# Attention plus FFN on one core: score matmuls in four column tiles, scores computed further ahead, row maxima turned by TensorE

## The reference

```python
xn = layernorm(x)                                  # x: (2, 1024, 128)
Q, K, V = heads(xn @ wq.T), heads(xn @ wk.T), heads(xn @ wv.T)   # 16 heads of 8 channels
Q, K = rope(Q), rope(K)
scores = where(causal, (Q @ K.T) / sqrt(8), -inf)  # 1024 x 1024 for each of 32 (batch, head) pairs
attn_out = (softmax(scores) @ V) -> (2, 1024, 128) @ wo.T
ffn_out = (xn @ CB.T) * (SCB / 127) + bias
y = x + attn_out + ffn_out
```

## Time and profile before

| | us |
|---|---|
| median of 3 runs | 286.92 |
| lowest, highest | 285.4, 288.29 |
| profiled execution | 285.84 |
| its span, first to last instruction | 284.1 |

### The profile page before, as it was taken

How to read it: one execution, slowest core, us unless ns; L and a number is a source line. 1 busy time by engine, 2 the same in 40 slices (tenths; PEclk the granted TensorE clock), 3 DMA queues, 4 the chain that set the end, 5 groups by cost and what they waited for, 6 DMA issues and landing times.

```text
span 284.1 us, 6851 instructions
## 1 busy us (share of the span) xinstructions
PE 254.6 (90%) x1734; PEld 111.1 (39%) x1760; DVE 217.6 (77%) x618; ACT 186.5 (66%) x350; POOL 108.0 (38%) x179
## 2 busy tenths in 40 slices
PE   0695849679999999999999999999999999998984
PEld 0342815333334334432433343334334432464553
DVE  5898368999898888979897898889888979732123
ACT  0326343566778868787777777687868786677851
POOL 6616999838625104500430043025104500640020
PEclk9999799999999999999999999999999999999996
DMA  7514767400660500150033004200500000001011
GB/s 200 179 35 132 212 132 151 119 2 4 141 155 25 155 16 1 45 125 1 0 85 85 0 1 119 51 0 10 157 4 0 1 1 0 3 20 39 18 39 37
DMA packets 22614, 17.76 MB, mean 63 GB/s; under 512 B 4148, under 2 KB 21940, under 8 KB 22600
## 3 DMA queue, kind: packets, MB, share of 16 engines
q1 hardware_dynamic: 22024, 17.00, 23.6%
q10 hardware_dynamic: 576, 0.59, 0.9%
HBM read 12.12 MB, written 5.24 MB: 61 GB/s over the span
## 4 chain that ended last, share of the span: by engine, by line
PE 77%; DVE 8%; DMA 4%; SPq 3%; issue 2%; POOL 2%; ACT 1%
PE psV L841 25%; PE psB L817 24%; PE psA L796 21%; DVE prod L665 4%; PE psA L891 3%; DMA k_scratch<-ot 2%; SPq L273 2%; DMA x_sb<-x 1%; DVE xn L623 1%; SPq L287 1%; DMA ks<-k_scratch 1%; PE psA L910 1%; PE psB L778 1%; DVE prod L650 1%; DVE stats L613 1%
## 5 line engine op out<-in xcount | busy, mean ns | idle before, releaser
L665 DVE CUSTOM_DVE_ANT_0 prod<-psA,cmask 128x128 f32<-128x128 f32 (+7 forms) x256 | 180.5, 754 | 34.4 <-PE psA L796 32.9
L564 ACT ACTIVATE ring<-psB 128x512 f32<-128x512 f32 x288 | 156.6, 602 | 53.7 <-PE psB L817 52.5
L796 PE MATMUL psA<-ks,qs 128*128 (+4 forms) x375 | 88.3, 327 | 9.3 <-DVE mx L665 5.9
L433 POOL TENSOR_SCALAR_AFFINE_SELECT ring<-ring 128x512 f32<-128x512 f32 x64 | 42.1, 670 | 138.5 <-ACT ring L564 138.3
L817 PE MATMUL psB<-qs,ks 128*128 (+4 forms) x367 | 92.6, 326 | 1.6 <-issue 1.1
L841 PE MATMUL psV<-ring,va 128*32 128x512 f32 (+3 forms) x768 | 78.5, 496 | 0.6 <-ACT ot L571 0.6
L817 PEld LDWEIGHTS psB<-qs,ks 128*128 (+1 forms) x384 | 33.2, 97 | 69.9 <-issue 28.7
L796 PEld LDWEIGHTS psA<-ks,qs 128*128 (+1 forms) x384 | 33.1, 98 | 40.2 <-DVE mx L665 11.1
L841 PEld LDWEIGHTS psV<-ring,va 128*32 128x32 f32 x768 | 16.8, 108 | 29.7 <-issue 19.2
L665 DVE DVE_READ_ACCUMULATOR2_ANT mx<- 128x1 f32 x256 | 21.3, 83 | 0.0
L713 DVE TENSOR_TENSOR xn<-psA,x_sb 128x256 f32<-128x256 f32 x6 | 2.5, 425 | 16.1 <-PE psA L910 16.1
(11 more groups left out here) (80 smaller groups left out, 153.4 us busy)
## 6 DMA issues: line engine op xcount, KB each, us to landing
qs<-q_scratch SPq DMA_DIRECT2D x48, 96.0 KB
ks<-k_scratch SPq DMA_DIRECT2D x48, 96.0 KB
q_scratch<-ot SPq DMA_DIRECT2D x20, 128.0 KB, 2.4
k_scratch<-ot SPq DMA_DIRECT2D x12, 128.0 KB, 2.4
x_sb<-x SPq DMA_DIRECT2D x4, 256.0 KB, 4.8
rope_sb<-rope SPq DMA_DIRECT2D x2, 512.0 KB, 6.2
qs<-shiftsT SPq DMA_DIRECT2D x64, 2.0 KB
y<-xn SPq DMA_DIRECT2D x8, 128.0 KB, 1.8
```

The costliest lines, as they stand in the source:

```text
L433: pool.affine_select(out=view, in_=view, compare_op=ALU.is_ge, fill=0.0, base=0, pattern=[[0, QUAD], [1, P]], channel_multiplier=-1).then_ ...
L564: act.activation(ring[:, s % P_RING, k * HALF:(k + 1) * HALF], bank_b(n % B_RING), ACT.Exp)\
L665: last = dve.tensor_tensor_reduce(masked_scores[:, u % 2, at:at + w], psA[:, (u % 2) * SEQ + at:(u % 2) * SEQ + at + w], cmask[:, SEQ - w: ...
L796: mm = pe.matmul(psA[:, (u % 2) * SEQ + at + k:(u % 2) * SEQ + at + min(k + HALF, w)], stack(qs, i, j, t * P, P), stack(ks, i, j, k, min(H ...
```

## The change

- Each score tile, in `scores` and in `shifted`, is no longer one matmul with 128 columns of weights but four with 32, each into its own 32 output partitions (`score_tile`), the same streamed operand four times.
- `UNIT_BANK` is new: the first three units of a quad come before the first bank of the quad before it (for quad 1 they stand in the prologue), the last comes after bank 28 in place of 34. `VALUE_BANK`, `LAST_VALUE_BANK`, `TASKS`, `TASK_AFTER` and `EARLY` are new too.
- The maxima are turned by a float32 matmul against the identity, with the 16 columns of `mx` as weights. It takes a place of its own in the ring of `psB` banks after banks 13 and 33 (`turn_in_ring`); ScalarE copies the 16x128 result out (`save_maxima`); GpSimd splits it with two operations in place of three; two DMAs in place of four store it. The VectorE transpose goes. Minus one stands in the key stack in place of a negated maximum. For quad 0 two tasks do the turning.
- No engine has a hardware loop any more: every program is written out for all eight quads, and every wait has a constant.
- In the prologue GpSimd fills the pads of slot 2 and the mask before the late rotations; the split of late parts 6 and 7 moves into quad 0; the addition of the FFN result moves from quad 0 to quad 1, in four pieces.

```diff
-UNIT_BANK = [1, 2, 4, 6, 7, 9, 10, 12, 14, 15, 15, 19, 20, 21, 23, 24, 25, 26, 27, 30, 32, 34]
-VALUE_BANK = [9, 14, 17, 20, 23, 25, 31, 35, 39, 42]
-LAST_VALUE_BANK = [9, 12, 14, 17, 20, 24, 28, 33, 37, 39]
+UNIT_BANK = [-5, -3, -1, 0, 3, 4, 5, 9, 10, 10, 11, 13, 13, 16, 18, 20, 20, 22, 23, 24, 27, 28]
+MAXIMA_BANK = [13, 33]
+VALUE_BANK = [10, 13, 16, 20, 23, 27, 31, 36, 40, 43]
+LAST_VALUE_BANK = [10, 12, 15, 20, 22, 25, 28, 33, 37, 39]
-EARLY = {1: 0, 6: 1, 12: 2, 18: 3, 24: 4, 29: 5}
+EARLY = {10: 0, 14: 1, 18: 2, 22: 3, 26: 4, 29: 5}
-TASKS = [("late", 4), ("late", 5), ("v", 0), ("v", 1), ("late", 6), ("late", 7), ("ffn", 0), ("ffn", 1)]
+TASKS = [("late", 4), ("late", 5), ("v", 0), ("v", 1), ("ffn", 0), ("ffn", 1), ("late", 6), ("max", 0), ("late", 7),
+         ("max", 1)]
...
             def split_maxima(i, hf):
...
-                pool.tensor_scalar(shifts[:, hf, 0:16], mx[:, hf, :], -1.0, None, ALU.mult).then_inc(split_step, 1)
-                pool.wait_ge(split_step, 2 * n + 1)
-                pool.tensor_tensor(mrest[:, hf, :], mx[:, hf, :], shifts[:, hf, 0:16], ALU.add).then_inc(split_step, 1)
-                wait(pool, split_step, 2 * n + 2, alone=True)
-                pool.tensor_scalar(shifts[:, hf, 16:32], mrest[:, hf, :], -1.0, None, ALU.mult).then_inc(shift_split, 1)
+                pool.tensor_copy(high, maxT[:, hf, :]).then_inc(split_step, 1)
+                pool.wait_ge(split_step, n + 1)
+                pool.tensor_tensor(low, maxT[:, hf, :], high, ALU.subtract).then_inc(shift_split, 1)
...
+            def save_maxima(i, hf):
+                e = ring_place(i - 1, MAXIMA_BANK[hf]) + 1
+                act.wait_ge(b_filled, e + 1)
+                act.wait_ge(shift_split, 2 * i + hf - 1)
+                act.activation(maxT[:, hf, :], bank_b(e % B_RING)[0:16, 0:P], ACT.Copy).then_inc(exp_done, 1)
...
-            def turn_shifts(i, hf):
-                wait(dve, shift_split, 2 * i + hf + 1)
-                wait(dve, shift_in[hf], i * (16 * SHIFT_DMAS))
-                dve.transpose(shiftsT[:, hf, :], shifts[:, hf, :]).then_inc(shift_turned[hf], 1)
...
+            def score_tile(psum, at, size, keys, queries):
+                for strip in range(0, P, STRIP):
+                    mm = pe.matmul(psum[strip:strip + STRIP, at:at + size], keys[:, strip:strip + STRIP], queries,
+                                   start=True, stop=True)
+                return mm
...
-                        mm = pe.matmul(psA[:, (u % 2) * SEQ + at + k:(u % 2) * SEQ + at + min(k + HALF, w)],
-                                       stack(qs, i, j, t * P, P), stack(ks, i, j, k, min(HALF, w - k)),
-                                       start=True, stop=True)
+                        size = min(HALF, w - k)
+                        mm = score_tile(psA, (u % 2) * SEQ + at + k, size, stack(qs, i, j, t * P, P), stack(ks, i, j, k, size))
...
+            def turn_maxima(i, hf, to):
+                pe.wait_ge(a_drained, i * NUNITS + (NUNITS if hf else HALF_UNITS))
+                return pe.matmul(to[0:16, 0:P], mx[:, hf, :], ident[:, :], start=True, stop=True)
+            def turn_in_ring(i, hf):
+                e = ring_place(i - 1, MAXIMA_BANK[hf]) + 1
+                wait(pe, exp_done, e - B_RING + 1)
+                turn_maxima(i, hf, bank_b(e % B_RING)).then_inc(b_filled, 1)
...
-                    mm = pe.matmul(out_bank[:, col:col + size], stack(ks, i, j, b * P, P),
-                                   stack(qs, i, j, hf * HALF + q0, size), start=True, stop=True)
+                    mm = score_tile(out_bank, col, size, stack(ks, i, j, b * P, P), stack(qs, i, j, hf * HALF + q0, size))
...
-            for u in range(NUNITS):
-                scores(0, u)
-                if u in TASK_AFTER:
-                    task(*TASK_AFTER[u])
+            for i in range(2):
+                for u in range(NUNITS):
+                    if unit_bank(i, u) < 0:
+                        scores(i, u)
+                        if i == 0 and u in TASK_AFTER:
+                            task(*TASK_AFTER[u])
+            task(len(TASKS) - 1, 0)
             pe.wait_ge(task_saved, len(TASKS))
-            body(0, True, True)
-            with pe.Fori(1, QUADS - 1) as i:
-                body(i, False, True)
+            for i in range(QUADS - 1):
+                body(i)
```

More of the change, by code:

```diff
@@ L23 @@
 LOWEST = -3.0e38
-TWO_ONES = float(np.frombuffer(np.array([0x3F803F80], np.uint32).tobytes(), np.float32)[0])
+TWO_MINUS_ONES = float(np.frombuffer(np.array([0xBF80BF80], np.uint32).tobytes(), np.float32)[0])
 F32 = mybir.dt.float32
@@ L238, in attention_ffn_kernel, with wait, stack_loaded @@
         y_out = sem("y_out")
[L239 to L253, removed]
+        def wait(eng, semaphore, value):
+            if value > 0:
+                eng.wait_ge(semaphore, value)
+        def stack_loaded(i):
+            return 16 * (2 * PARTS * (i // SLOTS + 1) + i // SLOTS)
+        SHIFT_DMAS = 2
         ROUND_DMAS = 2 * PARTS + 2
@@ L297, in store_shifts @@
+                if i >= SLOTS:
+                    sp.dma_start(qs[SHIFT:SHIFT + NSHIFT, slot, hf, :, :],
+                                 qs[SHIFT + NSHIFT:SHIFT + 2 * NSHIFT, slot, hf, :, :]).then_inc(ready, 16)
             def store_shifts(i, hf):
                 slot = i % SLOTS
[L300 to L304, removed]
+                sp.wait_ge(shift_split, 2 * i + hf + 1)
@@ L424, in mask @@
                 buf = ring[:, s % P_RING, :]
-                wait(pool, exp_done, i * NBANKS + BANK_END[s], alone=True)
+                pool.wait_ge(exp_done, ring_place(i, BANK_END[s] - 1) + 1)
                 if kind == D2:
@@ L586, in copy_turned @@
                 act.activation(onT[:, g % 2, :], result_bank(g, 2)[:, 0:2 * P], ACT.Copy).then_inc(onT_ready, 1)
-            body(0, True)
-            with act.Fori(1, QUADS - 1) as i:
-                body(i, False)
             last = QUADS - 1
+            for i in range(last):
+                body(i)
             def beside(n):
@@ L660, in maximum @@
                 t, heads = UNITS[u]
-                wait(dve, a_filled, i * NUNITS + u + 1, alone=True)
+                dve.wait_ge(a_filled, i * NUNITS + u + 1)
                 for j in heads:
@@ L843, in values, with body @@
                 mm.then_inc(pv_done, 1)
-            def body(i, first, more, then=None):
+            def body(i, then=None):
+                last = i == QUADS - 1
                 for s in range(NSTEPS):
@@ L849, in body @@
                         shifted(i, s, k)
-                        if more:
+                        for ahead in (i + 1, i + 2):
                             for u in range(NUNITS):
-                                if UNIT_BANK[u] == n:
-                                    scores(i + 1, u)
+                                if ahead < QUADS and unit_bank(ahead, u) == i * NBANKS + n:
+                                    scores(ahead, u)
+                        if n in MAXIMA_BANK and not last:
+                            turn_in_ring(i + 1, MAXIMA_BANK.index(n))
                         for v in range(NSTEPS):
-                            if (VALUE_BANK if more else LAST_VALUE_BANK)[v] == n:
+                            if (LAST_VALUE_BANK if last else VALUE_BANK)[v] == n:
                                 values(i, v)
-                            elif VALUE_BANK[v] == NBANKS + n and not first:
+                            elif VALUE_BANK[v] == NBANKS + n and i > 0:
                                 values(i - 1, v)
@@ L925, in _ @@
             pe.wait_ge(cb_scaled, 4)
-            body(QUADS - 1, False, False, then=early)
+            body(QUADS - 1, then=early)
             values(QUADS - 1, NSTEPS - 2)
```

311 lines of the change are left out of this document (153 added, 158 removed).

## The result

The changed kernel takes 292.93 us (median of 4 runs, 292.5 to 293.45); the kernel before, on the same chip beside it, 287.25 us (4 runs, 285.4 to 288.29). The ratio is 1.0206, 95% interval 1.0149 to 1.0262: slower by 2.1%, and outside the range.

What follows compares the result with a forecast made beforehand. TensorE was taken to set the loop, at 26.58 us a quad. Seven quads -13.7, prologue +2.9 and -1.0, quad 7 +2.3 sum to -9.5 us: 276.3, or 277 on the runs' scale; range 268 to 290.

Steps and rivals of the forecast that it cites:

- term 3: Loop quads: units further ahead and no hardware loops save 0.2 us of 1.3 us of waits a quad.
- rival (d): Loop: TensorE is freed but the order of buffers and masks holds; above 25.7 us a quad, 283 to 287 us; 10%.
- terms 4 and 5: Prologue: first exponential +2.9 us, columns done early -1.0; quad 7: changes of shape and waits for ScalarE, +2.3 us.
- term 1: Score tiles: four column tiles stream side by side, so changes of shape around value groups go; -2.2 us a quad.
- term 2: Turning the maxima: two more float32 matmuls on TensorE, 0.22 us each, +0.44 us a quad.
- (a): Score tiles: each pays its first weight load of 25 ns, +2.4 us a quad; about 295 us; 7%.
- (b): TensorE issue: sustained issue is slow, 25 ns an instruction, +4.5 us a quad; some 310 us; 6%.
- (c): TensorE array: it still empties between forms, so quads stay at 26.6 + 0.44 us; 292 to 295 us; 4%.
- no wait: Turns at banks 13 and 33: the units they need finished by banks 4 and 28, so TensorE needn't wait.
- Just hidden: Quad 0, bank 10: second half's shifts land at 68 us as the bank comes; up to 3 us if not.
- Instruction fetching: Written-out programs: 2.5 times the instructions stay hidden unless fetches are serial with issue; 7 packets of 16 KB before.

Runs made afterwards that it cites:

- e2: The kernel before with its five hardware loops written out and nothing else: 282.12 us, ratio 0.9823.
- e3: e2 with score tiles in four columns, the old order and the old way of turning: 279.82 us, ratio 0.9756.
- e1: The changed kernel with each score tile one 128x128 matmul again: 304.27 us, ratio 1.0576.
- f4: e4 with whole tiles in quad 0's scores too and the stores of quad 1's second shifts ahead of SyncE's wait: 267.76 us, ratio 0.9361.
- h2: g4 with the second half's maxima turned after bank 2 of their own quad, and quad 0's second turn after its bank 3: 273.26 us, ratio 0.9537.
- f1: The changed kernel with the old banks of units and values, turns after banks 15 and 35: 290.99 us, ratio 1.0166.
- g2: f4 with the units spaced as the change spaces them, six banks later (1 to 34): 287.98 us, ratio 1.006.
- g3: f4 with the change's VALUE_BANK only: 283.23 us, ratio 0.9896.
- g1: f1 with every unit two banks earlier (-1 to 32), value groups unmoved: 299.23 us, ratio 1.0438.
- f3: The changed kernel with whole tiles in quad 7 and the old EARLY and LAST_VALUE_BANK: 289.48 us, ratio 1.0114.
- e4: e3 with whole tiles in quad 7's scores: 275.98 us, ratio 0.9629.
- g4: f1 with whole tiles in quad 0's scores and in quad 7, and the old EARLY and LAST_VALUE_BANK: 284.47 us, ratio 0.9928.
- f2: The changed kernel with UNIT_BANK spaced as before but four banks earlier (-3 to 30), values as changed: 287.53 us, ratio 1.0056.

## Why the prediction was wrong

The step that failed is term 3: "The units spread over banks -5 to 28 … Of the 1.3 us of waits I take 0.2 (bounds 0 and 1.3)". I took a gain where the order brought a loss, and excluded a loss without a reason. It is the mechanism of rival (d), the order that holds, to which I gave 10%; and terms 4 and 5 were too small by 3.0 and 3.3 us, which took the time past that rival's 287 too.

| per loop quad | forecast | measured | from |
|---|---|---|---|
| term 1, tiles | -2.2 | -2.17, -2.20 | e2 to e3, e1 to after |
| term 2, two turns | +0.44 | +0.56 | f4 to h2 |
| term 3, no loops | in the -0.2 | -0.49 | before to e2 |
| term 3, new order | in the -0.2 | +1.7 | after, 26.17, less 24.46 of h2 |

The first three rows are steps of one chain of runs (before, e2, f4, h2), which ends at 24.46. The last is the rest between that and 26.17. It is measured against the old order with the turns where they wait for nothing; against f1, where the second turn waits 1.5 us behind the last unit, the new order is only 0.17 us slower. No run has the change's order without turns.

**Term 1** held in both orders: the earlier trace rows were read rightly, and the columns, the loads and the count of instructions cost nothing. Rivals (a), (b) and (c) fall with the rows at 172.00 to 173.79. The upper bound that the Trainium skill made likelier (TensorEngine Tiling (Array Packing), Gotcha 2: Feature Incompatibilities), 0.055 us on each 128-column tile, doesn't show: two such tiles and two of 384 columns take 0.44 us, 0.427 of it columns.

**Term 2**: 0.28 us a turn in place of 0.22. The forecast "no wait" was right for the change's banks 13 and 33, which the order had paid for, and wrong as a statement about turns: behind the last unit one costs 1.5 us (f1). Turning the maxima on TensorE bought nothing: f4 keeps VectorE's transpose and its quads are the shortest.

**Term 3, the loops.** "Register work costs TensorE nothing that shows" was drawn from quad 0, 26.66 us, against 26.58 of the loop. But quad 0 has other work: VectorE 23.87 us in place of 22.66, GpSimd 14.30 in place of 6.88. Its equal length hid a gain; e2 shows 0.49 us. Nor were "the other 1.3 us a quad" all waits: 0.49 of them went with the loops, and f4 still has 23.90 - 23.04 = 0.86 us above its columns with TensorE busy throughout. Start to start, a tile of 512 columns takes 216 ns there and one of 128 takes 56, some 3 ns above their columns each; what the rest is stays open.

**Term 3, the order.** That 22.9 us of VectorE's work in 24.6 leaves slack was right as a sum and said nothing about hand-over. There are two halves of `psA` and 22 units; a unit may start when the unit two before it is drained, and in between TensorE must have banks or values to do that last as long. g2 and g3 show that units alone (+2.9 us) and values alone (+2.0) spoil it, with all counts equal, and g1 that shifting the same units by two banks adds 1.1 us while it removes a wait of 1.5. The two costs don't add up to the 1.7 us of the change; g2 has the change's spacing six banks later, though, so the change's two lists never ran together without turns, and how they act on each other stays open.

**Term 4** allowed for a first exponential at 61.4 us, and 64.37 came. Before, the first bank started at 58.14, 1.8 us ahead of the end of quad 0's last maxima (59.92). Now it stands behind it, as the chain shows:

```profile
59.95 1.23 DVE prod L677
61.24 1.68 PE psA L784 x20
62.92 0.43 PE psB L804 x2
63.38 0.28 ACT maxT L529
63.70 0.62 PE psB L784 x4
```

What I counted (unit 2's drain, a turn, ScalarE's copy) is there. The gain of 1 us from moved tasks isn't: VectorE ends its maxima at 61.18, 1.3 us later than before, though the first score tile starts at 32.5 in both. From there to the bank it takes 2.5 us, 0.5 more than I had. The turn ahead of the first bank is the dear part: h2, which moves it, gains at most 5.0 us there, of which quad 0 gives 1.2 back. "Just hidden" at bank 10 was right for the change; in h2, where the banks begin earlier, it is late by 0.5 us.

Two other causes look likely, and the traces don't bear them out here. The slow clock: f3 has the same prologue, at 2.4 GHz until 63.1 us, and takes 31.8 us from its first score tile to its first exponential (33.51 to 65.34), as the change does (32.52 to 64.37) with 8.1 us at 1.2 GHz. Where the change has 1.68 us of TensorE in the chain, f3 has 0.85 us of VectorE and 0.82 of TensorE. The shape of the tiles, 128x128 tasks between tiles of 32 columns: in the old prologue it costs (58.29 to 62.99 from e2 to e3, 63.35 to 58.56 from e4 to f4; a slow stretch of 3.4 us came or went with it, which at half the clock can be at most 1.7 us of the 4.7). In the change's it doesn't show: e1, with whole tiles, has 64.02, and g4 is no sooner than f1.

**Term 5.** The cost of shape was right: 4.4 - 2.6 = +1.8 us forecast (two of the 12 value groups stand behind the last score tile and save nothing, so 2.2 at this rate), 2.0 measured (e3 to e4) and 1.9 (e1 to after, 32.66 to 34.57). The order was the error: 0.5 us forecast for `EARLY`, 3.7 measured (e1's 32.66, whole tiles, against 28.95). Half of this is `EARLY` and `LAST_VALUE_BANK`: f3 takes them back and has 30.78, 1.9 less. The other half, which the prediction has nowhere, comes with `VALUE_BANK`, whose last groups of quad 6 reach into quad 7: with that list old too, g4 has 28.74. The waits of TensorE for VectorE's `on` in the rows above are its sign.

**Instruction fetching** The earlier trace rows rose from 7 packets to 32 and cost nothing that shows: f4 fetches 30 and has TensorE busy throughout its quads.

Still open: which pair of units makes each wait; why the clock fell in the change's prologue and not in f2's trace with the same idle times; and whether a better order than the old one exists, since only five lists were run.

## What to carry to other kernels

An edit that shortens one engine's work and an edit to a hand-written order are two changes: run the first in the old order before touching the second. Where engines hand buffers over in turns, compare the time to drain one with the work that stands between the two uses, place by place; the sum of busy time says nothing about it. If a hand-made list is to be changed, price it from both sides of zero, since here a list of 22 numbers was worth 2.9 us of 24. And before an idle or slow stretch of one engine is blamed for a late stage, look whether the chain runs through it.

## What the runs showed of the hardware

- Matmuls in different column tiles that stream the same operand start 3 ns apart and run side by side in bfloat16 too: 8 instructions in 56 ns for 128 columns. A matmul with 16 columns of weights takes one such tile and lets the others go on: after the first turn's pass at 179.33 three tiles of the value group start at once,

```profile
179.33 0.27 PE L804 MATMUL psB<-ident,mx 128*16 128x128 f32 x1
179.33 0.52 PE L852 MATMUL psV<-ring,va 128*32 128x384 f32 x3
179.44 0.27 PE L804 MATMUL psB<-ident,mx 128*16 128x128 f32 x1
```

- The Trainium skill (TensorE: Matmul & The Clock Gate, Back-to-back issue gap) has a floor of 25 ns between matmul starts. Across column tiles it doesn't hold here. Starts in different tiles lie 2 to 4 ns apart, and a whole unit of four 128-column tiles, 16 matmuls, takes 0.22 us in the changed kernel, 14 ns each:

```profile
191.70 0.22 PE psA L784 x16
191.92 0.86 PE psV L852 x8
```

- TensorE fell to 1.2 GHz in the prologue for 3.4, 6.8 or 10.2 us, in some versions and executions and not in others. In e3 it had worked 0.27 of 3.40 us and was then at 0.50 for 3.4 us. In the change's prologue this cost nothing that shows, because VectorE set the pace; the row of the clock alone doesn't price a slow stretch.
